# When the weight matrices are cast to bf16 for the scratch copy: all seven at the start, or two at the start and five behind the first K and V projections

## The chip, the cores and the metric

The kernel runs on all 8 cores of one Trainium2 chip. Each core computes two of the 16 sequences, and no core waits for another. The metric is the device time of the slowest core in microseconds.

A core has five engines with programs of their own: PE (matmuls), ACT (activations), DVE (vector work), POOL and SP (here both only issue transfers). They run side by side and meet through semaphores. 16 DMA engines do all transfers of the core.

## The reference, cut to what matters

For every sequence x of 2048 rows and 1024 columns, attention with 16 heads of 64, a residual and a layer norm, then a feed-forward block with a token shift, a residual and a layer norm:

```python
q, k, v = x @ Wq, x @ Wk, x @ Wv                  # per head
attn = softmax(q @ k.T / 65536)
x = layernorm(x + (attn @ v) @ WO)
xr = mu_r * x + (1 - mu_r) * x_prev               # x_prev: x one row earlier
xk = mu_k * x + (1 - mu_k) * x_prev
r = sigmoid(xr @ W_r.T)
x = layernorm(x + r * (square(relu(xk @ W_k.T)) @ W_v.T))
```

Seven weight matrices of 1024 x 1024 come in as float32 in one tensor `wts`, in the order WK, WV, WQ, WO, FR, FK, FV (0 to 6).

## The kernel before

All matmuls run in bf16. A weight matrix in bf16 fills one of three slots of 2 MB in SBUF. `WS[2]` holds WQ for the whole run. `WS[0]` and `WS[1]` are reloaded over and over, 36 times in all, from `wsc`, a bf16 copy of the matrices in device memory that the kernel makes itself at its start.

**The head.** POOL issues the load of a small constant and of WQ. Then a loop over m = 0 to 6 makes the scratch copy: POOL loads matrix m into `WS[m % 2]` with a cast from float32 to bf16, and SP writes the slot out to `wsc`. From m = 2 on POOL first waits until the slot's earlier write is done (counters `c_ws0` and `c_ws1`), and SP waits for each cast (`c_wc0`, `c_wc1`):

```python
for m in range(7):
    slot = WS[m % 2]
    if m >= 2:
        wait("g", c_wsx[m % 2], c_wsx[m % 2].n)
```

**Weight loads.** `load_weight(mat)` takes the slots 0 and 1 in turn. SP issues the load from `wsc`; the very first call waits for both counters of the scratch copy (`scratch_all`), and each call waits until the last matmul that reads the slot is done (`slot_free`).

**Per sequence.** `emit_kv` computes K and V for the whole sequence in four blocks of 512 rows, in the order 1, 2, 3, 0. Of each block it runs 64 matmuls for K with slot 0 and 64 for V with slot 1; results go through four PSUM banks and DVE writes them as bf16. The x blocks are loaded with a cast by POOL into two buffers in turn (`ABA`, `RG`), each issued during the K pass before it. Behind that come four stages t = 0 to 3, one for each block of 512 query rows: Q projection (`q_group`), then attention over 8 pairs of heads and 16 key tiles (`emit_attention`), in which PE computes scores, ACT the exps, PE the sums. Into the attention of stage t are woven the layer norm and the feed-forward work of stage t - 1 (`fillers`). The output projection of stage t - 1 (`emit_wo_pairs`, weights WO, residual from the tile `Y1`) stands at the start of stage t.

In stage t = 0 of the first sequence nothing is woven in. SP issues there the x tile for `Y1` and, behind it, the load of WO; POOL issues the x block for the next stage (`XRA`).

**What sets the order.** Each engine works through its own list in program order. A waiting POOL or SP therefore holds back every later transfer that it issues. The names that matter below: SP's list in the head is seven scratch writes, the reloads of WK and WV (`load_weight`), the x tile for `Y1`, then WO. POOL's list is WQ, seven casts, four x blocks of `emit_kv`, the block for `XRA`. Line 93 of the profile is every DMA issue, 99 every matmul, 109 every activation, 118 every vector operation, 84 every wait, since all are recorded by helpers.

Of the kernel before, what the change touches and what calls it, by code (L numbers as in the profile page):

```python
# [24 lines left out]
WK, WV, WQ, WO, FR, FK, FV = range(7)  # L25
# [8 lines left out]
def build_nc():  # L34
# [13 lines left out]
    def em(eng, fn):  # L48
        plan[eng].append(fn)

    def C(name):
        c = Cnt(name)
        sems[name] = c
        return c
# [6 lines left out]
    c_ws0 = C("c_ws0")  # L61
    c_ws1 = C("c_ws1")
# [9 lines left out]
    c_g = C("c_g")  # L72
# [7 lines left out]
    def wait(eng, c, val=None):  # L80
        v = c.n if val is None else val
        if v <= 0:
            return
        em(eng, lambda e, _n=c.name, _v=v: e.wait_ge(sem_handles[_n], _v))

    def bump(c, by=1):
        c.n += by
        return c.n

    def dma(eng, dst, src, c):  # L90
        n = bump(c, 16)
        em(eng, lambda e, _d=dst, _s=src, _n=c.name:
           e.dma_start(_d, _s).then_inc(sem_handles[_n], 16))
        return n

    def mm(out, lhsT, rhs, start, stop, tp=None, inc=None):
        n = bump(inc) if inc is not None else None
        def f(e, _o=out, _l=lhsT, _r=rhs, _st=start, _sp=stop, _tp=tp, _inc=inc):
            i = e.matmul(_o, _l, _r, start=_st, stop=_sp, tile_position=_tp,  # L99
                         skip_group_check=True)  # L100
            if _inc is not None:
                i.then_inc(sem_handles[_inc.name], 1)
        em("t", f)
        return n
# [10 lines left out]
    def vop(name, args, inc=None):  # L115
        n = bump(inc) if inc is not None else None
        def f(e, _nm=name, _a=args, _inc=inc):
            i = getattr(e, _nm)(*_a)  # L118
            if _inc is not None:
                i.then_inc(sem_handles[_inc.name], 1)  # L120
        em("v", f)
        return n
# [6 lines left out]
    with contextlib.ExitStack() as ctx:  # L129
# [54 lines left out]
        def next_bank():  # L184
            if use4[0]:
                b = pool4[hidx[0] % 4]
                hidx[0] += 1
            else:
                b = bG[gidx[0] % 2]
                gidx[0] += 1  # L190
            acquire(b)
            return b
# [96 lines left out]
        c_wc = [c_wc0, c_wc1]  # L289
        c_wsx = [c_ws0, c_ws1]  # L290
        c_w = [c_w0, c_w1]
        for m in range(7):
            slot = WS[m % 2]
            if m >= 2:
                wait("g", c_wsx[m % 2], c_wsx[m % 2].n)
            nld = dma("g", bass.AP(slot, 0, [[8 * D, 128], [D, 8], [1, D]]),
                      bass.AP(wts, m * D * D, [[D, 128], [128 * D, 8], [1, D]]),
                      c_wc[m % 2])
            wait("s", c_wc[m % 2], nld)
            dma("s", bass.AP(wsc, m * D * D, [[D, 128], [128 * D, 8], [1, D]]),  # L300
                bass.AP(slot, 0, [[8 * D, 128], [D, 8], [1, D]]), c_wsx[m % 2])

        wnext = [0]
        scratch_all = [(c_ws0, c_ws0.n), (c_ws1, c_ws1.n)]
# [3 lines left out]
        def load_weight(mat):  # L308
            si = wnext[0]
            wnext[0] = 1 - si  # L310
            if first_load[0]:
                wait("s", scratch_all[0][0], scratch_all[0][1])
                wait("s", scratch_all[1][0], scratch_all[1][1])
                first_load[0] = False
            fa = slot_free[si]
            if fa is not None:
                wait("s", fa[0], fa[1])
            n = dma("s", bass.AP(WS[si], 0, [[8 * D, 128], [D, 8], [1, D]]),
                    bass.AP(wsc, mat * D * D, [[D, 128], [128 * D, 8], [1, D]]),
                    c_w[si])  # L320
            return si, n
# [16 lines left out]
        for seq in range(NSEQ):  # L338
            def emit_kv(kv_fillers):
                use4[0] = True  # L340
                wk_si, wk_n = load_weight(WK)
                wv_si, wv_n = load_weight(WV)
                wk_last = wv_last = 0
                wait("t", c_w[wk_si], wk_n)
                wait("t", c_w[wv_si], wv_n)
                order = (1, 2, 3, 0)
                dsts = {1: ABA, 2: RG, 3: ABA, 0: RG}
                buf_free = {id(ABA): (c_g, xb_free[0]), id(RG): None}
                loads = {}

                def emit_load(tb):
                    buf = dsts[tb]
                    wait("g", c_xb, c_xb.n)
                    fa = buf_free[id(buf)]
                    if fa is not None:
                        wait("g", fa[0], fa[1])
                    loads[tb] = dma(
                        "g",
                        bass.AP(buf, 0, [[NCH * QT, 128], [QT, 8], [1, QT]]),
                        bass.AP(xT, seq * D * S + tb * QT,  # L360
                                [[S, 128], [128 * S, 8], [1, QT]]), c_xb)

                emit_load(1)
                for idx, tb in enumerate(order):
                    buf = dsts[tb]
                    nxb = loads[tb]
                    if tb == 0:
                        kv_nxb0[0] = nxb
                    wait("t", c_xb, nxb)
                    xbch = [buf[:, k * QT:(k + 1) * QT] for k in range(8)]  # L370
                    for hp in range(NHP):
                        b = next_bank()
                        for k in range(8):
                            mm(b.ap[:, :],
                               WS[wk_si][:, k * D + hp * 128: k * D + (hp + 1) * 128],
                               xbch[k], start=(k == 0), stop=(k == 7),
                               inc=(c_g if k == 7 else None))
                        wk_last = c_g.n
                        wait("v", c_g)
                        nv = vop("tensor_copy",  # L380
                                 (KTB[:, hp * S + tb * QT: hp * S + (tb + 1) * QT],
                                  b.ap[:, :]), inc=c_vg)
                        b.free = (c_vg, nv)
                    if kv_fillers:
                        kv_fillers.pop(0)()
                    if idx + 1 < len(order):
                        if buf_free[id(RG)] is None:
                            buf_free[id(RG)] = (c_g, c_g.n)
                        emit_load(order[idx + 1])
                    for tt in range(4):  # L390
                        for half in range(2):
                            b = next_bank()
                            for k in range(8):
                                mm(b.ap[:, :], xbch[k][:, tt * 128:(tt + 1) * 128],
                                   WS[wv_si][:, k * D + half * 512:
                                             k * D + half * 512 + 512],
                                   start=(k == 0), stop=(k == 7),
                                   inc=(c_g if k == 7 else None))
                            wv_last = c_g.n
                            kti = tb * 4 + tt  # L400
                            wait("v", c_g)
                            nv = vop("tensor_copy",
                                     (VTB[:, kti * D + half * 512:
                                          kti * D + half * 512 + 512],
                                      b.ap[:, :]), inc=c_vg)
                            b.free = (c_vg, nv)
                    if kv_fillers:
                        kv_fillers.pop(0)()
                    buf_free[id(buf)] = (c_g, wv_last)
                    xb_free[0] = wv_last  # L410
                slot_free[wk_si] = (c_g, wk_last)
                slot_free[wv_si] = (c_g, wv_last)
                while kv_fillers:
                    kv_fillers.pop(0)()
                use4[0] = False
# [4 lines left out]
            if prev is not None:  # L420
# [3 lines left out]
                kvf = [lambda: emit_ln1_head(prev),  # L424
                       lambda: (emit_ln_bcast_apply(prev, Y1)[0], emit_mix(prev))]
            emit_kv(kvf)

            wait("v", c_va, c_va.n)
# [646 lines left out]
```

## Time and profile before

| | us |
|---|---|
| median of two runs | 2720.14 (2711.89 and 2728.40) |
| the profiled execution, its own time | 2707.63 |
| its span on the slowest core (core 4) | 2706.1 |
| spans of the eight cores | 2693.5 to 2706.1 |
| PE busy | 2075.5 (77%) |
| ACT busy | 1244.6 (46%) |
| DVE busy | 835.1 (31%) |
| mean granted clock of PE | 0.897 |

Times within the trace count from the start of the span. "Busy" of PE and of the other engines is work only; waits and the issuing of transfers are not in it. The DMA share is the mean busy share of the 16 DMA engines and can come out a little above 1, since their packets overlap. A row such as "ws<-wts" names the destination and then the source. The load of a weight matrix or an x block with a cast counts by the bytes that it writes.

### The profile page before, as it was taken

Reading aid. Unit: us, or ns where it says so; the run is one execution under the profiler, and the core shown is the slowest. Engines: PE = TensorE matmul, PEld = TensorE weight load, DVE = VectorE, ACT = ScalarE, POOL = GpSimd, SP = SyncE. Lnnn points to the kernel's source line nnn. Section 1 sums busy time; section 2 is a strip of 40 time slices with the busy share of each in tenths; the row PEclk is TensorE's granted clock in tenths of the full one; section 3 lists DMA queues with packets and bytes.
Section 4 is the critical chain, followed back from the end, with each engine's and each line's share of the span. In section 5 each row is a group of like instructions: output and inputs, shape, how many; then the busy total and the mean of one; then the engine's idle time right before and its main releaser. Section 6 shows DMA issues by size and latency. Waiting matters only on the chain.

```text
span 2706.1 us, 29989 instructions; the slowest of 8 cores (2693.5 to 2706.1 us)
## 1 busy us (share of the span) xinstructions
PE 2075.5 (77%) x10062; PEld 709.2 (26%) x10176; DVE 835.1 (31%) x1369; ACT 1244.6 (46%) x1441; POOL 20.1 (1%) x27
## 2 busy tenths in 40 slices
PE   0019988788878897889669888788988798879835
PEld 0004322222322232223224222222322232223212
DVE  0003200240524052405264014240434133423355
ACT  0000277375537653665200656457445655565511
POOL 0000000000000000000000000000000000000000
PEclk9999988898989898889779999898988898889867
DMA  9984100000410041003222013100230013001201
GB/s 175 205 196 63 63 1 1 32 1 32 109 63 1 32 109 63 1 32 94 78 31 48 31 63 79 63 1 1 75 110 19 1 63 110 31 1 63 94 31 63
DMA packets 85136, 157.24 MB, mean 58 GB/s; under 512 B 1984, under 2 KB 16384, under 8 KB 84992
## 3 DMA queue, kind: packets, MB, share of 16 engines
q1 hardware_dynamic: 53264, 107.07, 12.4%
q0 software_dynamic: 23024, 31.47, 8.0%
q10 hardware_dynamic: 8704, 16.78, 1.7%
q8 instruction: 91, 1.49, 0.2%
q14 instruction: 53, 0.43, 0.1%
HBM read 155.31 MB, written 31.46 MB: 69 GB/s over the span
## 4 chain that ended last, share of the span: by engine, by line
PE 54%; ACT 19%; DVE 11%; DMA 7%; issue 7%; ACTq 1%; DVEq 0%; POOL 0%; SPq 0%; POOLq 0%
PE psg L99 28%; ACT pb L109 13%; PE pspv L99 11%; PE psden L99 10%; ACT lta L109 4%; DMA ws<-wts 4%; PE psa L99 3%; PE psb L99 3%; DMA wsc<-ws 3%; DVE xka L118 2%; DVE stv L118 2%; DVE rg L118 1%; DVE xra L118 1%; DVE recb L118 1%; ACT rcr L109 1%
## 5 line engine op out<-in xcount | busy, mean ns | idle before, releaser
L109 ACT ACTIVATE pb<-psa 128x1024 bf16<-128x1024 f32 x512 | 522.6, 1021 | 396.6 <-PE psa L99 395.4
L109 ACT ACTIVATE pb<-psb 128x1024 bf16<-128x1024 f32 x512 | 523.5, 1022 | 362.7 <-PE psden L99 192.6
L99 PE MATMUL pspv<-pb,vtb 128*64 128x512 bf16 x2048 | 427.5, 426 | 23.0 <-DVE aba L118 22.9
L99 PE MATMUL psden<-pb,cstb 128*32 128x512 bf16 x2048 | 410.5, 409 | 0.0
L99 PE MATMUL psg<-xra,ws 128*128 128x512 bf16 x1264 | 343.2, 422 | 9.3 <-issue 8.6
L99 PE MATMUL psa<-qtb,ktb 64*128 64x512 bf16 x1024 | 213.6, 405 | 144.6 <-ACT pb L109 84.6
L118 DVE TENSOR_TENSOR aba<-pspv,rsb 128x512 bf16<-128x512 f32 x64 | 44.3, 692 | 767.9 <-ACT rsb L109 766.8
L99 PE MATMUL psg<-aba,ws 128*128 128x512 bf16 x373 | 95.4, 409 | 218.7 <-DMA ws<-wsc 190.9
L99 PE MATMUL psb<-qtb,ktb 64*128 64x512 bf16 x1024 | 207.6, 399 | 62.4 <-ACT pb L109 62.4
L99 PEld LDWEIGHTS pspv<-pb,vtb 128*64 128x64 bf16 x2048 | 110.7, 109 | 283.6 <-issue 283.6
L99 PEld LDWEIGHTS psg<-xra,ws 128*128 128x128 bf16 x1320 | 128.6, 105 | 199.5 <-issue 94.6
L99 PEld LDWEIGHTS psden<-pb,cstb 128*32 128x32 bf16 x2048 | 93.8, 94 | 250.3 <-issue 250.3
L109 ACT ACT_TABLE_LOAD x1 | 1.3, 1283 | 306.4 <-PE psa L99 306.4
L99 PEld LDWEIGHTS psa<-qtb,ktb 64*128 64x128 bf16 x1024 | 53.0, 93 | 301.8 <-issue 300.9
L99 PE MATMUL psg<-rcr,cstf 64*128 64x512 f32 x128 | 83.4, 736 | 57.9 <-ACT rcr L109 57.9
L99 PEld LDWEIGHTS psg<-aba,ws 128*128 128x128 bf16 x384 | 39.7, 104 | 273.8 <-issue 236.0
L99 PEld LDWEIGHTS psb<-qtb,ktb 64*128 64x128 bf16 x1024 | 52.6, 93 | 214.8 <-issue 214.8
L99 PE MATMUL psg<-xka,ws 128*128 128x512 bf16 x465 | 105.6, 379 | 2.3 <-issue 2.2
L118 DVE CAST qtb<-psg 128x512 bf16<-128x512 f32 x60 | 41.5, 691 | 173.6 <-PE psg L99 173.6
L118 DVE CAST ktb<-psg 128x512 bf16<-128x512 f32 x32 | 22.0, 691 | 230.3 <-PE psg L99 229.3
L118 DVE TENSOR_SCALAR stv<-psg 128x512 f32<-128x512 f32 x30 | 20.7, 691 | 223.4 <-PE psg L99 223.4
L109 ACT ACTIVATE rsb<-psg 128x512 f32<-128x512 f32 x64 | 38.2, 597 | 98.9 <-PE psg L99 98.9
(113 smaller groups left out, 1695.9 us busy)
## 6 DMA issues: line engine op xcount, KB each, us to landing
ws<-wsc SPq DMA_DIRECT2D x36, 2048.0 KB, 10.1
ws<-wts POOLq DMA_DIRECT2D x8, 2048.0 KB, 25.8
y<-xT SPq DMA_DIRECT2D x8, 2048.0 KB, 13.2
outT<-outb ACTq DMA_DIRECT2D x32, 512.0 KB, 4.0
wsc<-ws SPq DMA_DIRECT2D x7, 2048.0 KB, 12.5
xra<-xT POOLq DMA_DIRECT2D x6, 1024.0 KB, 12.2
aba<-xT POOLq DMA_DIRECT2D x4, 1024.0 KB, 13.6
rg<-xT POOLq DMA_DIRECT2D x4, 1024.0 KB, 8.9
```

The source lines that it names most:

```text
L99: i = e.matmul(_o, _l, _r, start=_st, stop=_sp, tile_position=_tp, skip_group_check=True)
L109: i = e.activation(_o, _i, _f, scale=_s, bias=_b)
L118: i = getattr(e, _nm)(*_a)
```

## The change

The loop becomes a function, `emit_wcast(m)`, with the same two transfers and one more wait. It is called for matrices 0 and 1 (WK and WV) at the old place, and for 2 to 6 behind the K and V projections of the first sequence. Those projections no longer call `load_weight`: they read WK and WV in the slots into which they were cast, and PE waits for the two casts. The casts of matrices 2 to 6 wait, besides the slot's earlier scratch write, for the last K matmul (slot 0) or the last V matmul (slot 1). The scratch counters on which the first `load_weight` waits, now that of WO in stage t = 0, are set again behind the last cast. For the second sequence nothing changes.

```diff
-        for m in range(7):
+        kv0_gate = [0, 0]
+
+        def emit_wcast(m):
             slot = WS[m % 2]
             if m >= 2:
                 wait("g", c_wsx[m % 2], c_wsx[m % 2].n)
+                wait("g", c_g, kv0_gate[m % 2])
             nld = dma("g", bass.AP(slot, 0, [[8 * D, 128], [D, 8], [1, D]]),
                       bass.AP(wts, m * D * D, [[D, 128], [128 * D, 8], [1, D]]),
                       c_wc[m % 2])
             wait("s", c_wc[m % 2], nld)
             dma("s", bass.AP(wsc, m * D * D, [[D, 128], [128 * D, 8], [1, D]]),
                 bass.AP(slot, 0, [[8 * D, 128], [D, 8], [1, D]]), c_wsx[m % 2])
+            return nld
+
+        wk0_n = emit_wcast(0)
+        wv0_n = emit_wcast(1)
...
             def emit_kv(kv_fillers):
                 use4[0] = True
-                wk_si, wk_n = load_weight(WK)
-                wv_si, wv_n = load_weight(WV)
+                if seq == 0:
+                    wk_si, wv_si = 0, 1
+                    wait("t", c_wc[0], wk0_n)
+                    wait("t", c_wc[1], wv0_n)
+                else:
+                    wk_si, wk_n = load_weight(WK)
+                    wv_si, wv_n = load_weight(WV)
+                    wait("t", c_w[wk_si], wk_n)
+                    wait("t", c_w[wv_si], wv_n)
                 wk_last = wv_last = 0
-                wait("t", c_w[wk_si], wk_n)
-                wait("t", c_w[wv_si], wv_n)
...
                 slot_free[wk_si] = (c_g, wk_last)
                 slot_free[wv_si] = (c_g, wv_last)
+                if seq == 0:
+                    kv0_gate[0], kv0_gate[1] = wk_last, wv_last
+                    for m in range(2, 7):
+                        emit_wcast(m)
+                    scratch_all[0] = (c_ws0, c_ws0.n)
+                    scratch_all[1] = (c_ws1, c_ws1.n)
```

## Rows read from the trace of the kernel before

**Rows 1.** The page's chain that ended last, by engine and by line.

```profile
PE 54%; ACT 19%; DVE 11%; DMA 7%; issue 7%; ACTq 1%; DVEq 0%; POOL 0%; SPq 0%; POOLq 0%
PE psg L99 28%; ACT pb L109 13%; PE pspv L99 11%; PE psden L99 10%; ACT lta L109 4%; DMA ws<-wts 4%; PE psa L99 3%; PE psb L99 3%; DMA wsc<-ws 3%; DVE xka L118 2%; DVE stv L118 2%; DVE rg L118 1%; DVE xra L118 1%; DVE recb L118 1%; ACT rcr L109 1%
```

**Rows 2.** That chain in order of time: start us, us, what.

```profile
3.14 29.92 DMA ws<-wts
...
33.13 18.38 DMA wsc<-ws
...
116.20 19.45 DMA wsc<-ws
...
136.18 22.45 DMA ws<-wts
...
158.69 11.86 DMA wsc<-ws
...
171.10 19.60 DMA ws<-wsc
190.70 0.24 issue
190.94 5.24 PE psg L99 x16
```

**Rows 3.** Busy time by stretch (the busy engines, clock, DMA share, GB/s).

```profile
0.00:191.00 191.00, 0.06 (x1) 0.09 (x2) 3.50 (x1) 0.00 (x0) 8.78 (x14) 1.00 1.00 197
191.00:305.00 114.00, 113.44 (x510) 51.11 (x520) 44.38 (x72) 0.00 (x0) 3.49 (x4) 1.00 0.32 67
194.00:337.00 143.00, 139.83 (x662) 59.99 (x672) 49.91 (x80) 20.13 (x21) 3.49 (x4) 1.00 0.28 61
337.00:500.00 163.00, 139.78 (x711) 39.57 (x713) 6.82 (x10) 119.78 (x133) 0.00 (x0) 0.85 0.00 1
207.00:217.00 10.00, 9.95 (x47) 4.53 (x47) 3.80 (x6) 0.00 (x0) 0.87 (x1) 1.00 0.68 107
305.00:313.00 8.00, 6.70 (x38) 2.25 (x38) 2.08 (x3) 4.55 (x5) 0.00 (x0) 1.00 0.75 262
```

**Rows 4.** SP's and POOL's issues in order of time: start, us, engine, what.

```profile
48.92 0.36 SPq L93 DMA_DIRECT2D wsc<-ws  x1
158.69 0.36 SPq L93 DMA_DIRECT2D wsc<-ws  x1
289.50 0.36 SPq L93 DMA_DIRECT2D ws<-wsc  x1
171.77 6.57 SPq L93 DMA_DIRECT2D y<-xT  x1
137.04 0.88 POOL L93 DMA_DIRECT2D aba<-xT  x1
```

**Rows 5.** Issues of short stretches: KB, us to landing (at 48.92, 137.04, 171.1, 171.8, 207.09).

```profile
wsc<-ws SPq DMA_DIRECT2D x1, 2048.0 KB, 12.0
aba<-xT POOLq DMA_DIRECT2D x1, 1024.0 KB, 29.2
ws<-wsc SPq DMA_DIRECT2D x1, 2048.0 KB, 19.6
y<-xT SPq DMA_DIRECT2D x1, 2048.0 KB, 24.2
rg<-xT POOLq DMA_DIRECT2D x1, 1024.0 KB, 9.6
```

**Rows 6.** Spans and clocks, and core 0's first matmuls in order of time.

```profile
core 0: 2704.1 us, clock 0.897
core 4: 2706.1 us, clock 0.897
187.85 5.80 PE L99 MATMUL psg<-aba,ws 128*128 128x512 bf16 x16 [187.85 <-DMA ws<-wsc]
```

**Rows 7.** POOL's issues in order of time, with the idle time before each.

```profile
52.05 0.88 POOL L93 DMA_DIRECT2D ws<-wts  x1 [47.14 <-DMA wsc<-ws]
...
93.75 0.87 POOL L93 DMA_DIRECT2D ws<-wts  x1 [31.42 <-DMA wsc<-ws]
...
136.18 0.87 POOL L93 DMA_DIRECT2D ws<-wts  x1 [31.49 <-DMA wsc<-ws]
...
207.09 0.87 POOL L93 DMA_DIRECT2D rg<-xT  x1 [69.17 <-PE psden L99]
```

**Rows 8.** PE and DVE in order of time, at the end of stage t = 0.

```profile
492.25 2.86 PE L99 MATMUL psg<-aba,ws 128*128 128x512 bf16 x7 [2.23 <-DVE aba L118]
497.02 0.69 DVE L118 TENSOR_TENSOR outb<-psg,y 128x512 f32<-128x512 f32 x1 [5.50 <-PE pspv L99]
507.04 1.89 PE L99 MATMUL psg<-xra,ws 128*128 128x512 bf16 x8
```

**Rows 9.** ACT in order of time, first attention steps.

```profile
308.60 1.02 ACT L109 ACTIVATE pb<-psb 128x1024 bf16<-128x1024 f32 x1
...
316.66 1.02 ACT L109 ACTIVATE pb<-psa 128x1024 bf16<-128x1024 f32 x1
```

## The prediction

> **What bounds the kernel now.** I read the page's chain by engine and line first [rows 1]: PE holds 54% of the chain, but "DMA ws<-wts" 4% and "DMA wsc<-ws" 3% are on it too, and a transfer on the chain is time in which nobody computes. The chain in order of time shows where [rows 2]: from 3.14 us to 190.94 us it is only transfers, a weight matrix into SBUF, out to the scratch copy `wsc`, the next one in, four times over, then the reload of two matrices, and only then the first matmul at 190.94. The stage table says the same [rows 3]: in 0 to 191 us PE is busy 0.06 us and the 16 DMA engines are full (share 1.00); in 191 to 305 us, the K and V projections of sequence 0, PE is busy 113.44 of 114 us. So the head is bound by DMA, the projections behind it by PE, and the attention stages behind those by PE and ACT in turn. PE is in fixed program order and everything behind the first matmul waits for it directly or indirectly, so an earlier first matmul moves the rest as a block, unless something in that block then meets a transfer that comes too late.
>
> **The change part by part.**
>
> Removed from the head: the casts of matrices 2 to 6, their scratch writes, and the reload of matrices 0 and 1. The K and V projections take their weights straight from the slots into which they were cast. What they now wait for is three transfers: WK, WV and the first x block.
>
> WK is in at 33.1 us and WV at 48.9: SP waits for exactly these landings before it issues each scratch write, and the issues stand at 33.13 and 48.92 [rows 2, 4]. Up to there the new program issues the same transfers in the same order, so both numbers carry over.
>
> The first x block now follows WV directly on POOL's queue. The trace has the same pair: the block is issued at 137.04 behind the last matrix, that matrix is in by 158.69 (the issue of its scratch write), and the block lands 29.2 us after its own issue, at 166.2 [rows 4, 5]. That is 7.5 us behind the matrix, with a scratch write of 2 MB running beside it as it will in the new head. One thing is different: at 48.9 the scratch write of WK still runs, until 33.13 + 18.38 = 51.5 us [rows 2], which at worst puts 2.6 us of full DMA ahead of the block. So the block lands between 48.9 + 7.5 = 56.4 and 59.0; I take 58, towards the upper end since the engines are full, and the first matmul there. (A landing releases PE within 0.24 us: 171.10 + 19.60 against 190.94 [rows 2].) Gain on core 4: 190.9 - 58 = 132.9 us. On core 0, which starts at 187.85 and has a span of 2704.1, the gain is 129.9, and its span becomes 2574.2; core 4's becomes 2706.1 - 132.9 = 2573.2 [rows 6]. The slowest core then stands at about 2574.
>
> The HBM page of the Trainium skill (HBM Reference, Specifications) gives about 358 GB/s a core with both cores of a pair streaming. As an estimate from that page, three float32 matrices and one block, 14.7 MB, would be in after 41 us, at about 44, and the sum would be 14 us lower; the trace does not agree, it has only the three matrices (12.6 MB) in at 48.9, some 280 GB/s, and I go by the trace.
>
> The K and V projections themselves: 114 us as before. Their later x blocks are issued by POOL ahead of the moved casts, so nothing new is queued before them. The only transfer still running at their start is the scratch write of WV, 12 us long from 48.92 on [rows 5]; the second x block is issued 16 us behind the first matmul [rows 7], at about 74, when this write is over. Cost 0.
>
> Moved behind the projections: five casts and five scratch writes. POOL's cast of matrix 2 waits for the last K matmul, which today releases SP's reload at 289.50 [rows 4], so 289.5 - 132.9 = 156.6. The first of them has the engines nearly alone; from then on the pair period is that of the head, 41.7 and 42.4 us from matrix 2 to 4 to 6 (POOL's issues at 52.05, 93.75 and 136.18) [rows 7]. Only slot 1 opens later, with the last V matmul at 303.1 - 132.9 = 170, and matrix 3 must be queued at 170 instead of 9 us behind matrix 2; it still goes in while matrix 2 is written out. In: matrix 2 at about 173 (WV took 48.92 - 33.13 = 15.8 us), written by 192 (18.4 to 19.5 us), matrix 4 issued at 192, matrix 6 at 234 (one period), in at 256.5 (22.45 us), written at 268.4 (11.86 us) [rows 2].
>
> What is queued behind them. On SP: the x tile for `Y1`, which today is issued at 171.77 and needs 24.2 us, now goes out at 257 and is in at 281; then WO, which waits for both scratch counters (268.4) and needs 19.6 us, in at 288 [rows 4, 5]. On POOL: the x tile for the next stage (`XRA`), behind the cast of matrix 6, issued at 235 and in by 235 + 29.2 = 264. Who waits: the output projection of stage t = 0 has its first matmul at 492.25 today, so 359.3; the first sum with `Y1` is at 497.02, so 364.1; the first matmul on `XRA` at 507.04, so 374.1 [rows 8]. Slack: 71 us for WO, 83 for `Y1`, 110 for `XRA`. The cover is the attention stage t = 0, some 185 us with no transfer of its own (DMA share 0.00 in 337 to 500 us [rows 3]). Cost 0; with the cover gone it would be 1 us for every us beyond 71.
>
> Beside other work: the moved traffic fills the DMA engines (share 1.0) for about 112 us of attention. No stretch of before has both at full. The nearest: 207 to 217 us has DMA at 0.68 with PE busy 9.95 of 10; 305 to 313 us has DMA at 0.75 in the first attention steps [rows 3], and the exps there take 1.02 us each, as at 316.66 us with that load over [rows 9]. Bound below: nothing. A gain is excluded, since traffic lends no engine anything. Bound above: 8 us, 5% of the stage, for what a share of 1.0 might do that 0.75 doesn't. I take 0, since the row at 0.75 shows none.
>
> Sum: span 2706.1 gives 2574 for the slowest core; around it lay 2707.6 - 2706.1 = 1.5 us, so 2575.7 by the profiled execution. The two runs of before are 2711.9 and 2728.4, median 2720.1, some 4 to 21 us above the profiled one; less 132 the median would give 2588. Between the two I say **2580**.
>
> **The rivals.**
>
> *The first x block comes after the scratch write, not beside it.* If the engines favour the write of WV (over at about 61.5), the block of 9.6 us [rows 5] lands near 71, 13 us later: 2593. For it: the engines are full. Against it: at 158.69 to 170.6 the same two ran side by side and the block was in first.
>
> *The clock.* Granted clock is 1.00 from 194 to 337 us and 0.85 from 337 to 500 [rows 3], that is a mix of 2.4 and 1.2 GHz that begins 143 us behind PE's start. If that full stretch is earned by the 191 us of idling within the program, 58 us of idling would earn 58/191 of it, 44 us. The other 70 us of projections at 0.85 would take 12 us more, and the attention up to the old turning point some 4 more: 2596. Against it: PE was idle before the program too, and the stretch may simply count from PE's start, in which case it moves along.
>
> *The scratch copy is late.* Decides when WO lands past 359, that is when casts and writes take over 183 us instead of 112. At half the rate (224) WO lands at 400 and it costs 41 us: 2621; at a third (336) 153 us, and the whole gain is gone. Against it: rates are those of the head, where the engines did nothing else either.
>
> *Slower than before: PE and ACT suffer from the full DMA engines.* Place: the attention stage from 157 to 268 us. Each per cent is 1.1 us; the gain of 132 is eaten when the 112 us of work take 244, a factor of 2.2, and it is over 2% slower (2774 and up) from a factor of 2.7. Against it: at a share of 0.68 PE lost nothing [rows 3]. The Trainium skill (SBUF — State Buffer, SBUF: two separate sides) holds engine ports and DMA ports to be separate, so that neither slows the other; by that rule this rival would have no chance at all, and no run here shows it at a share of 1.0.
>
> **How the numbers follow.** My forecast 0.81, its own range 2563 to 2596 (landing 56.4 to 59.0, contention 0 to 8, and the 13 us between the two bases). Late x block 0.06, clock 0.06, late scratch copy 0.04, engines slowed 0.03. A range of 2562 to 2604 takes in the first three and leaves out the rest and the odd tail. About 2% is what a measurement of this kernel can tell from no change, so faster means under 2666: forecast, x block, clock, and half of the scratch rival, 0.95; within 2%: the other half and a third of the last, 0.03; slower 0.02.
>
> **What would show it.** First matmul at 56 to 60 us on core 4, released by the x block and not by a weight. PE busy over 99% in the next 114 us. Clock 1.00 until about 201 us. POOL's casts from 156 on with periods near 42 us, DMA share near 1.0 until 268, then WO at about 288. The first output projection at 359, not released by a DMA. From there on every stage 133 us earlier with its old length. I am wrong if the output projection waits for WO or `Y1`, if the clock falls long before 201 us, or if the exps between 157 and 268 us come further apart than they do now between 305 and 400.

## The result

| | before | after |
|---|---|---|
| time, median | 2712.31 us (10 runs) | 2584.01 us (11 runs) |
| profiled execution: its time, its span | 2707.63, 2706.1 | 2583.61, 2582.1 |
| ratio of the undisturbed runs | 1 | 0.953, 95% interval 0.9505 to 0.9555 |

The kernel is 128 us faster, 4.7%. The forecast was 2580. In some executions the cores of one die run at a lower clock and take longer; the two medians hold these too (without them they are 2711.9 and 2583.6), the ratio and all times below do not.

The page of the changed kernel, chain by engine: the share of DMA fell from 7% [rows 1] to 1%, and a 2% part appears that the chain cannot name. It is the wait for the first x block, 61 us long, as the row of PE shows further down.

```profile
PE 58%; ACT 20%; DVE 11%; issue 7%; another core or an unknown queue 2%; ACTq 1%; DMA 1%; DVEq 0%; POOLq 0%
```

The chain in order of time on core 3, the slowest (start us, us, what). Where before stood casts, writes and a reload one behind the other up to 190.94 [rows 2], one wait is left:

```profile
0.00 61.45 another core or an unknown queue
61.45 0.14 issue
61.58 6.21 PE psg L99 x16
```

Matmuls in order of time, the first on cores 3 and 4. The bracket names the idle time before and what ended it: the x block in `ABA`, no weight.

```profile
61.58 6.21 PE L99 MATMUL psg<-aba,ws 128*128 128x512 bf16 x16 [61.58 <-DMA aba<-xT]
61.94 5.01 PE L99 MATMUL psg<-aba,ws 128*128 128x512 bf16 x16 [61.94 <-DMA aba<-xT]
```

Stages of the changed kernel on core 3 (start and end, length, busy PE, weight loads, DVE, ACT, POOL, clock, DMA share, GB/s). They answer to [rows 3]: first the K and V projections with the end of the head, then the stretch of full clock, then attention with the moved casts beside it.

```profile
58.00:172.00 114.00, 110.42 (x500) 49.55 (x501) 42.70 (x62) 0.00 (x0) 3.50 (x4) 1.00 0.31 52
61.00:204.00 143.00, 141.08 (x660) 60.35 (x660) 49.91 (x80) 15.63 (x16) 5.24 (x6) 1.00 0.45 82
204.00:370.00 166.00, 142.18 (x727) 40.12 (x726) 6.82 (x10) 124.34 (x138) 2.62 (x3) 0.87 0.59 124
```

PE is busy in 110.42 of the 110.42 us that remain of the first stretch behind 61.58. The clock is 1.00 for 143 us from the start of PE and 0.87 in the stretch behind it; before, it was 1.00 from 194 to 337 and then 0.85 [rows 3]. Read in steps of 1 us, it first falls 147 to 149 us behind the first matmul on the eight cores, and 146 to 148 us in the kernel before.

POOL's and SP's issues on core 3 in order of time. They answer to [rows 4, 7]: the casts now stand behind the projections, a matrix pair every 38.1 and 42.7 us, and the reload of WO is issued at 278.44.

```profile
4.86 0.91 POOL L93 DMA_DIRECT2D aba<-xT  x1
...
161.57 0.87 POOL L93 DMA_DIRECT2D ws<-wts  x1 [40.57 <-PE psden L99]
175.38 0.87 POOL L93 DMA_DIRECT2D ws<-wts  x1 [12.94 <-PE psden L99]
199.63 0.87 POOL L93 DMA_DIRECT2D ws<-wts  x1 [23.37 <-DMA wsc<-ws]
210.85 0.87 POOL L93 DMA_DIRECT2D ws<-wts  x1 [10.35 <-DMA wsc<-ws]
242.36 0.87 POOL L93 DMA_DIRECT2D ws<-wts  x1 [30.63 <-DMA wsc<-ws]
243.22 0.88 POOL L93 DMA_DIRECT2D xra<-xT  x1
```

```profile
50.78 0.36 SPq L93 DMA_DIRECT2D wsc<-ws  x1
264.80 0.36 SPq L93 DMA_DIRECT2D wsc<-ws  x1
265.25 0.57 SPq L93 DMA_DIRECT2D y<-xT  x1
278.44 1.39 SPq L93 DMA_DIRECT2D ws<-wsc  x2
```

The end of stage t = 0 on core 4, PE in order of time: the output projection is still released by DVE and not by a transfer, with the same idle time of 2.23 us as in [rows 8].

```profile
360.53 3.19 PE L99 MATMUL psg<-aba,ws 128*128 128x512 bf16 x7 [2.23 <-DVE aba L118]
```

**Where the time went.** Split each core's span at its first matmul. The head was 181.2 to 190.9 us long on the eight cores and is 60.2 to 62.4 now. The rest, from first matmul to the end, was 2512.4 to 2516.6 us, on average 2514.6, and is 2513.4 to 2520.5, on average 2517.0. So the head gave 121 to 129 us on a core, and the rest took 2.4 us back on average, more on core 3, where 2512.9 became 2520.5, and on core 7, where 2513.9 became 2520.5. The average rest of the kernels below that differ only in the head lies between 2512.4 and 2516.8, so 2.4 us is within what one execution and another differ by.

The spans and clocks of these two cores after the change:

```profile
core 3: 2582.1 us, clock 0.888
core 4: 2576.8 us, clock 0.891
```

Core 3's 7.6 us lie behind stage t = 0: from its first matmul to the output projection it took 487.74 - 187.94 = 299.8 us before and 362.16 - 61.58 = 300.6 after, and from there to the end 2213.1 and 2219.9. In that later part the two programs issue the same work, and core 4 shows no such difference (rest of 2515.2 before, 2514.9 after). The same 1300 us near the end, before and after on core 3 (columns of [rows 3]), show what it is:

```profile
1400.00:2700.00 1300.00, 1067.42 (x5140) 361.06 (x5140) 447.91 (x743) 638.27 (x746) 3.50 (x4) 0.88 0.16 49
1272.00:2572.00 1300.00, 1075.97 (x5140) 361.89 (x5140) 444.54 (x738) 639.02 (x746) 3.49 (x4) 0.87 0.15 48
```

PE is busy 8.6 us longer with the same number of matmuls, at a granted clock of 0.87 instead of 0.88; on core 7 it is 8.8 us with the same two clocks. So these microseconds go with the granted clock. Why it was lower on these two cores is not shown; I count it to the scatter between cores.

### The profile page after: what moved, and what is told of

It reads as the page before. It is cut to its first block, busy times and chain, and to the rows that moved or that the text cites. A ratio compares the mean times of both kernels' runs of the same rounds, so it can differ in the third digit from the quotient of the medians.

```text
span 2582.1 us, 30106 instructions; the slowest of 8 cores (2573.9 to 2582.1 us)
## 1 busy us (share of the span) xinstructions
PE 2103.9 (81%) x10176; PEld 710.7 (28%) x10176; DVE 834.9 (32%) x1369; ACT 1245.8 (48%) x1441; POOL 20.1 (1%) x27
## 4 chain that ended last, share of the span: by engine, by line
PE 58%; ACT 20%; DVE 11%; issue 7%; another core or an unknown queue 2%; ACTq 1%; DMA 1%; DVEq 0%; POOLq 0%
PE psg L99 29%; ACT pb L109 13%; PE pspv L99 11%; PE psden L99 11%; ACT lta L109 5%; PE psa L99 4%; PE psb L99 3%; DVE xka L118 2%; DVE stv L118 2%; DVE rg L118 2%; DVE xra L118 1%; DVE recb L118 1%; ACT rcr L109 1%; DVE y L118 1%
## 5 line engine op out<-in xcount | busy, mean ns | idle before, releaser
L99 PE MATMUL psg<-xra,ws 128*128 128x512 bf16 x1320 | 351.4, 419 | 0.3 <-issue 0.3
L109 ACT ACTIVATE lta<-psg 128x512 f32<-128x512 f32 x60 | 35.8, 596 | 65.0 <-PE psg L99 64.4
```

Of the source, the lines that this page charges most:

```text
L109: i = e.activation(_o, _i, _f, scale=_s, bias=_b)
```

## The experiments

Every kernel below starts from the changed one. "First matmul" is that of core 4 unless said otherwise, and a single core scatters by some 2 us, so averages over the eight cores are given where it matters.

### One part undone: the reload

```diff
-                if seq == 0:
-                    wk_si, wv_si = 0, 1
-                    wait("t", c_wc[0], wk0_n)
-                    wait("t", c_wc[1], wv0_n)
-                else:
-                    wk_si, wk_n = load_weight(WK)
+                wk_si, wk_n = load_weight(WK)
...
                     scratch_all[1] = (c_ws1, c_ws1.n)
+                    first_load[0] = True
```

> The changed kernel with one part undone: the casts of matrices 2 to 6 stay behind the first projections, but WK and WV are loaded once more from the scratch copy before the projections start, as in the kernel before. Theory (the head is a chain of transfers, each part worth its own transfers): both scratch writes are done near 64 us, the two reloads take about 20 us, so the first matmul stands near 84 instead of 61 us and the time is 2584 + 22 = 2606. So of the 128 us, about 106 come from moving the five casts and 22 from not reloading. Rival (the time is set by the body, the head is half hidden): under 5 us difference, 2585 to 2589. The stretch of full clock should again end 143 us behind the first matmuls, near 230 us, if it counts from PE's start; if idling within the program earns it, it would be longer than in the changed kernel.

Measured: 2604.2 us (one execution), first matmul at 81.94, released by the reload:

```profile
63.97 0.99 SPq L93 DMA_DIRECT2D ws<-wsc  x2
```

```profile
81.94 6.08 PE L99 MATMUL psg<-aba,ws 128*128 128x512 bf16 x16 [81.94 <-DMA ws<-wsc]
```

The head is additive: on core 4 the first matmul is 20.0 us later, and the time is 20.2 us more. Over the eight cores the first matmul is 21.9 us later (83.1 against 61.2) and the rest behind it 1.9 us shorter (2515.1 against 2517.0). So some 20 to 22 of the 128 us come from reading WK and WV where they were cast, and the other 106 to 108 from moving the five casts. Its busy table has clock 1.00 from 85 to 228 us and 0.87 behind:

```profile
85.00:228.00 143.00, 140.47 (x662) 60.18 (x672) 49.91 (x80) 19.40 (x20) 6.14 (x7) 1.00 0.46 87
228.00:300.00 72.00, 60.75 (x316) 16.61 (x314) 2.77 (x4) 56.11 (x63) 1.75 (x2) 0.87 1.02 218
```

In steps of 1 us the clock first falls 146 to 149 us behind the first matmul on the eight cores, as it does with first matmuls near 61 and near 187. The idling inside the program earns nothing, and the clock rival falls. That the stretch counts from PE's start, as I had argued, does not follow: up to there PE does the same work in all three kernels, so the fall can just as well belong to a place in the program, some 35 us behind the last V matmul. The kernels below in which PE has to wait speak for the place: where the waits add up to 12 to 16 us, it falls 163 to 167 us behind the first matmul.

### What the moved traffic costs: none of it, and twice of it

```diff
-                    for m in range(2, 7):
+                    for m in ():
...
-                    bass.AP(wsc, mat * D * D, [[D, 128], [128 * D, 8], [1, D]]),
+                    bass.AP(wsc, (mat % 2) * D * D, [[D, 128], [128 * D, 8], [1, D]]),
```

> The changed kernel with the moved work left out: no casts and scratch writes of matrices 2 to 6; every later weight load reads the scratch copy of WK or WV instead of its own matrix, so the computed values are those of other weights, while all matmuls, loads and waits stay. It shows what the moved traffic costs the attention beside it. Theory (full DMA engines slow nobody): first matmul near 61 us, first output projection 299 to 301 us behind it as in the changed kernel, time 2580 to 2585. Rival (they slow PE and ACT): the output projection comes 3 us or more earlier against the first matmul, time under 2578.

```diff
-                    for m in range(2, 7):
+                    for m in (2, 3, 4, 5, 2, 3, 4, 5, 6, 3):
```

> The changed kernel with ten casts and scratch writes behind the first projections instead of five (2, 3, 4, 5 done twice, then 6 and 3 again), so twice the traffic and a later WO. It prices the rival 'scratch copy late' and the rival 'engines suffer from full DMA engines'. Theory (cover with slack): the last write ends near 380 us, WO is in near 392, the output projection of stage t = 0 would start at 361 and so waits about 30 us: 2614. The attention steps in between keep their length to 1%. Rival (full DMA engines slow PE and ACT): the attention stage itself becomes longer, by 5 us or more beside the wait.

Measured: 2583.3 and 2584.5 us without the casts, 2614.5 and 2616.8 with twice as many. The attention of stage t = 0 on core 4, the same 187 us in three kernels: no casts, five casts (the change), ten casts. The columns are those of [rows 3].

```profile
165.00:352.00 187.00, 165.37 (x868) 49.40 (x866) 15.34 (x30) 134.38 (x146) 0.00 (x0) 0.92 0.06 22
```

```profile
165.00:352.00 187.00, 164.99 (x865) 49.32 (x866) 14.64 (x29) 135.44 (x148) 4.36 (x5) 0.91 0.71 151
```

```profile
165.00:352.00 187.00, 164.99 (x860) 49.10 (x861) 14.64 (x29) 134.41 (x147) 8.74 (x10) 0.90 1.02 194
```

The DMA share goes from 0.06 over 0.71 to 1.02, and PE does 868, 865 and 860 matmuls, ACT 146, 148 and 147 activations. From first matmul to output projection core 4 takes 361.66 - 63.83 = 297.8 us without the casts and 360.53 - 61.94 = 298.6 with them. A single core scatters by more than that. Over the eight cores the rest behind the first matmul is 2516.6 us on average without and 2517.0 with, and PE needs from its first matmul to the end of its work before the output projection 298.2 us on average with no casts, 298.5 with five, 298.5 with ten (the wait for WO taken off) and 298.8 in the kernel before, with 295.9 to 299.7 on single cores. So full DMA engines slow neither engine by as much as 1 us in this stage. (By the Trainium skill, SBUF — State Buffer, SBUF: two separate sides, engine and DMA ports cannot contend; here the trace agrees, up to a share of 1.02.)

The kernel without casts is not faster as a whole, since its first matmul came later, at 63.8 (63.4 against 61.2 over the eight cores). SP had no casts to wait for and issued the 2 MB x tile for `Y1` at 49.2, beside the x block; I take that for the cause, it was not tried by itself.

The price of a late scratch copy shows in the ten casts. The reload of WO is issued at 383.64 on core 4, and the longest waits of PE there are

```profile
PE psg L99 <- DMA aba<-xT: 61.3, 1, 61.3
PE psg L99 <- DMA ws<-wsc: 38.1, 1, 38.1
```

The second is 27.9 us on core 3, where that reload is issued at 373.02, and 26.1 to 40.8 us over the eight cores. The time is 30 to 33 us up. WO's issue moved by 105.7 us on core 4 (277.95 to 383.64), of which 38.1 became a wait, and by 94.6 on core 3 (278.44 to 373.02), of which 27.9 did. So 67.6 and 66.7 us cost nothing: the slack that I had put at 71 us is measured on two cores. Between the two, 11.1 us more of delay became 10.2 us more of wait.

### What sets the first matmul: the queue ahead of the x block, and the writes beside it

```diff
-        n_wq_res = dma("g", bass.AP(WS[2], 0, [[8 * D, 128], [D, 8], [1, D]]),
-                       bass.AP(wts, WQ * D * D, ...), c_wqr)
+        n_wq_res = [0]
...
                 emit_load(1)
+                if seq == 0:
+                    n_wq_res[0] = dma("g", bass.AP(WS[2], 0, ...), bass.AP(wts, WQ * D * D, ...), c_wqr)
```

> The changed kernel with POOL's load of WQ moved behind WK, WV and the first x block. Theory (the first matmul waits for everything that stands before the x block in POOL's queue): one matrix less before it, 14 to 16 us, first matmul near 46 us, time 2584 - 15 = 2569. Rival (the x block's landing is set by the scratch writes beside it and not by the queue ahead): the first matmul stays within 5 us of 61, time 2580 to 2584.

Measured: 2569.8 us (one execution), first matmul at 53.2 on core 4 and 50.8 on core 3. The time fell by 14 as expected, but not for the reason expected: over the eight cores the first matmul fell by 9.7 us only (61.2 to 51.5), and the other 4.6 are the rest behind it (2517.0 to 2512.4), which this edit should not change. That the time came out right is luck. The queue ahead counts, but a matrix less ahead is not 15 us. The scratch write of WK starts sooner too (20.51 instead of about 33) and so runs beside all of WV and the block; that this took the missing 5 us is argued and was not tried.

Next the writes. `emit_wwrite(m)` below is the scratch write alone, the `dma("s", ...)` of the removed lines:

```diff
-            wait("s", c_wc[m % 2], nld)
-            dma("s", bass.AP(wsc, m * D * D, ...), bass.AP(slot, 0, ...), c_wsx[m % 2])
+            if m >= 2:
+                wait("s", c_wc[m % 2], nld)
+                emit_wwrite(m)
...
                 emit_load(1)
+                if seq == 0:
+                    wait("s", c_xb, loads[1])
+                    wait("s", c_wc[0], wk0_n)
+                    emit_wwrite(0)
+                    wait("s", c_wc[1], wv0_n)
+                    emit_wwrite(1)
```

> The changed kernel with SP holding the scratch writes of WK and WV until the first x block is in. It prices the term that I had too small, the x block at 61.4 where 58 was forecast: WV came at 50.8 to 51.2 (forecast 48.9) and the block 10.7 us behind it (forecast 9.1). Theory (the writes take their share of the DMA engines from WV and the block): without them WV is in near 47 and the block near 55, first matmul 6 us earlier, time 2578. Rival (the block is bound by its own reads, the writes fit into gaps): first matmul within 1.5 us of 61, 2584.

Measured: 2572.9 and 2574.5 us, first matmul at 50.92, with the writes issued right behind:

```profile
50.92 1.00 SPq L93 DMA_DIRECT2D wsc<-ws  x2
```

11 us earlier on core 4 and 10.4 over the eight cores, where 6 were expected: the scratch writes of WK and WV, which nobody needs before stage t = 0, held up the start by that much. The rival that they fit into gaps falls. The landings of WV and the block on core 4, counted from their issues at about 4.0 and 4.9, divide it, first in the changed kernel, then here:

```profile
ws<-wts POOLq DMA_DIRECT2D x1, 2048.0 KB, 47.2
aba<-xT POOLq DMA_DIRECT2D x1, 1024.0 KB, 56.9
```

```profile
ws<-wts POOLq DMA_DIRECT2D x1, 2048.0 KB, 41.0
aba<-xT POOLq DMA_DIRECT2D x1, 1024.0 KB, 45.9
```

WV is in 6.2 us sooner, and the block follows it by 5.8 us instead of 10.6.

### Using it: a shorter head

The first diff builds on `wq_last`, in which WQ has left the head of POOL's list; each further one shows only what is new against the kernel ahead of it. First WK, the x block, WV and WQ in that order, with PE waiting for WV only before the first V pass:

```diff
-        wv0_n = emit_wcast(1)
+        wv0_n = [0]
...
                 emit_load(1)
+                if seq == 0:
+                    wv0_n[0] = emit_wcast(1)
+                    n_wq_res[0] = dma("g", ...)          # WQ
...
+                    if seq == 0 and idx == 0:
+                        wait("t", c_wc[1], wv0_n[0])
                     for tt in range(4):
```

> As in wq_last, but POOL's order is WK, first x block, WV, WQ, and PE waits for WV only before the first V pass. Theory: WK is in near 20 us and the block near 30, first matmul at 30. WV is in near 47, just before the V pass at 48. But the second x block is issued near 47 behind WQ, lands past 70, and is needed at 59: PE stalls about 12 us there. Sum: 2584 - 31 + 12 = 2565. Rival (no such stall, the queues serve the block first): 2553. Rival on the other side (the stall also lowers the clock): above 2570.

Measured: 2567.2 and 2568.8 us, first matmul at 31.0. PE's waits on core 4 show what took the place of the old one: the second x block, queued behind WQ, and a little WV.

```profile
PE psg L99 <- DMA rg<-xT: 11.6, 1, 11.6
...
PE psg L99 <- DMA ws<-wts: 2.9, 1, 2.9
```

The stall breaks the stretch of full clock too; these are the projections around it:

```profile
31.00:64.00 33.00, 29.68 (x126) 12.74 (x128) 10.60 (x16) 0.00 (x0) 0.88 (x1) 1.00 1.03 193
64.00:78.00 14.00, 2.73 (x7) 1.05 (x8) 0.47 (x1) 0.00 (x0) 0.87 (x1) 0.67 0.68 141
78.00:190.00 112.00, 109.92 (x520) 46.83 (x528) 38.85 (x64) 16.27 (x17) 3.50 (x4) 0.99 0.48 87
```

Then WQ behind the second x block:

```diff
                         emit_load(order[idx + 1])
+                        if seq == 0 and idx == 0:
+                            n_wq_res[0] = dma("g", ...)  # WQ
```

> POOL's order WK, first x block, WV, second x block (issued behind the first K pass), WQ; PE waits for WV before the first V pass. The difference to wk_x_wv_wq is that WQ stands behind the second block. Theory (the stall of 11.6 us there was the block queued behind WQ): first matmul at 30 as there, no wait for the second block, up to 3 us of wait for WV, time 2568 - 12 = 2556. The stretch of full clock, which there was broken by the stall after 34 us, runs 143 us from PE's start again. Rival (the block is slow whatever stands before it, since the scratch writes run beside it): the wait stays over 8 us, 2565.

Measured: 2556.4 to 2556.9 us, first matmul at 30.7. The wait for the second block fell from 11.6 to 4.5 us on core 4, not to nothing, and that for WV to 1.3; over the eight cores it fell from 8.6 to 12.9 us to 2.1 to 6.1 on four of them and to none on the other four. The time is as expected. The clock was not whole again on core 4: it is 0.94 from 30 to 69 us. On core 1, with a wait of 2.1 us, it is 1.00 there.

Next the scratch writes held until WV is in (`emit_wwrite` as above, behind waits for `c_wc[0]` and `c_wc[1]`):

> As wq_after_x2, and SP holds both scratch writes until WV is in. Theory (the writes cost the loads their share): first matmul near 28 instead of 30, no wait for WV (in near 42, needed at 46), but both writes now run beside the second block, issued near 45 and needed near 59; a write and a block side by side took 10 to 12 us, so it is just in time. Time 2556 - 5 = 2551. Rival (two writes beside the second block delay it past 59): a wait of up to 6 us there and no gain, 2556.

Measured: 2559.2 and 2559.3 us, no gain; 2576.7 in the execution of the trace, in which cores 0 and 1 took some 20 us more than the other six. First matmul at 25.9, 4.8 us earlier, but

```profile
PE psg L99 <- DMA rg<-xT: 8.9, 1, 8.9
```

instead of 4.5, and 6.0 to 8.9 us on all eight cores: the rival was right. The block was issued at 42.15 and both writes at 37.97, and they ran side by side. What the writes no longer cost the first block they cost the second.

So the second block has to be issued sooner; its buffer is free from the start. It goes out as soon as the first is in, and WQ behind it:

```diff
+                    emit_load(order[1])
+                    n_wq_res[0] = dma("g", ...)          # WQ
...
-                        emit_load(order[idx + 1])
+                        if not (seq == 0 and idx == 0):
+                            emit_load(order[idx + 1])
```

> POOL's order WK, first x block, WV, second x block issued as soon as the first is in (its buffer is free from the start), then WQ; SP holds both scratch writes until WV is in. The last kernel showed that the earlier first matmul (26 instead of 30 us) was given back to a wait of 8.9 us for the second block, which was issued only behind the first K pass. Theory (the block was late because it was issued late and then shared with two writes): it now follows WV directly, is in near 48 to 52, needed at 55, no wait; first matmul at 26; time 2557 - 4.5 - 4.5 - 1.3 = 2547. Rival (some other transfer takes its place: the third block behind WQ, needed near 84): a new wait of 3 us or more at the third block, 2550 or above.

Measured: 2546.0 us in the profiled execution, 2549.5 in the median; the four executions lie between 2546.0 and 2562.4; ratio to before 0.940, interval 0.931 to 0.950. That interval covers the 0.943 of `wq_after_x2`, so the step of 7 to 10 us between the two kernels is shown by the waits in the traces and not by the ratios. First matmul at 26.88, and no other transfer stands among PE's waits until the attention, on any of the eight cores. POOL issued the block at 27.28:

```profile
27.28 0.88 POOL L93 DMA_DIRECT2D rg<-xT  x1 [22.38 <-DMA aba<-xT]
```

Last, the block ahead of WK, and WK in two halves of 512 columns with a counter each, PE waiting for the second half before the fifth group:

```diff
+                    for h, c_ in ((0, c_wka), (1, c_wc0)):
+                        wkh.append(dma("g",
+                            bass.AP(WS[0], h * 512, [[8 * D, 128], [D, 8], [1, 512]]),
+                            bass.AP(wts, h * 512, [[D, 128], [128 * D, 8], [1, 512]]), c_))
...
+                        if seq == 0 and idx == 0 and hp == 4:
+                            wait("t", c_wc0, wkh[1])
```

> As x2_at_once, but the first x block goes ahead of WK, and WK comes as two casts of 512 columns each, so that PE begins with the first half. Theory: block in near 11, first half of WK near 18, first matmul at 18 instead of 26; WV in near 38 but needed at 34 (18 + 16): 4 us of wait; net 4 us faster than x2_at_once, 2543. Rival (rows of half the length load more slowly, or the waits for WV and the third block eat the gain): within 2 us of x2_at_once or slower.

Measured: 2545.7 to 2547.1 us, ratio 0.937, interval 0.929 to 0.946; not to be told from the kernel before it. First matmul at 19.98, 6.9 us earlier, of which 3.2 go into a wait for WV before the first V pass, where 4 were expected; the second half of WK is not waited for. The casts behind the projections are issued at 122.37 instead of 126.94, so 4.6 us reach that point on core 4; at the end of the run core 4 is 2 us ahead (2542.1 to 2544.1) and the slowest core not at all. Where they went was not tried.

## Why the prediction was right, point by point

**The head is a chain of transfers and the rest moves as a block.** Right. The rest behind the first matmul stayed within 2.4 us on average, and the reload alone gave back 20 us at the end for 20 to 22 us at the start.

**WK and WV carry over at 33.1 and 48.9.** WK right (33.42 on core 3); WV came at 50.8 on core 3 and 51.2 on core 4, 2 us later, and at 50.1 instead of 48.7 on average over the eight cores. Up to there the issues differ only in the x block queued behind WV; the write of WK beside it ran longer too, on core 4 23.2 us instead of 18.4. Which of the two did it was not tried. A part can be scatter: `no_casts` has the same head up to there and has WV in at 48.7 on core 4.

**The x block, 9.1 us behind WV, at 58.** Too small by 3.6 us: it came at 61.4, outside the stretch of 56.4 to 59.0 that I had given. Of the 3.6, WV's own landing is 1.9 and the block behind it 1.6 (10.7 us instead of 9.1). I took 7.5 us from a block that ran beside one write and added at most 2.6 for the tail of the other. That tail was longer: on core 4 the write of WK ran until 55.9, 4.7 us past WV. `write_later` measured what both writes cost the start: 11 us. The row from which I worked held such a write already, so its price could not be seen in it.

**The slowest core.** I forecast a span of 2574.2 for it, from core 0 with a rest of 2516.2. It was core 3 with a rest of 2520.5. So the miss of 7.9 us in the span is 3.6 for the block and 4.3 for the scatter of the rest. That 2580 was only 4 us off is luck: by the profiled execution alone the sum was 2575.7, 8 us short, and the 4 us that I added came from the scatter of two runs of the kernel before (2711.9 and 2728.4), not from anything in the change.

**Projections at full clock, 114 us.** Right: matrix 2's cast waits for the last K matmul and goes out at 161.57 on core 3, 100.0 us behind the first matmul; the same matmul released SP's reload 99.1 us behind it there before. On core 4 it is 98.8 against 98.6.

**Moved casts and slack.** Forecast: casts from 156.6, WO's reload issued at 268.4 with 71 us of slack. Measured 161.6 and 278.4; relative to the first matmul, 216.9 instead of 210.4. The slack held, and `double_casts` found its edge, at 67 us, within 5 us of the sum. The two do not quite mean the same: WO's issue was 6.5 us later than forecast against the first matmul, so by my sum some 64 would have been left.

**Full DMA engines cost nothing.** Right, and now shown at a share of 1.02 to under 1 us over eight cores, where before had only rows at 0.68 and 0.75. The exps between 170 and 340 us took 1.02 us each with none, five and ten casts.

**The rivals.** Late x block: the measured landing is 3.6 us from the forecast and nearly 10 from this rival. Clock: falls, by three starts; my counter-argument, that the stretch counts from PE's start, is not shown. I had also begun the stretch at 194, 3 us behind the first matmul at 190.94. Late scratch copy: its mechanism is real, its condition was not met. Slower: falls. The estimate from the HBM page of the Trainium skill (HBM Reference, Specifications), a block at about 44 us, did not come about, not even with the writes held back, where it was in at 50.9.

## What to carry to other kernels

Where the first matmul waits for transfers, list what stands ahead of each input in its queue and what runs beside it, and ask of each when it is needed: five casts and a reload were 128 us, and the order of WQ, WV, an x block and two writes another 34 to 38. Each time the first wait is shortened, look for the next input in program order; here it took the gain twice, until its own issue was moved. The transfers that moved under compute here cost nothing that could be measured as long as their slack held, and beyond it each microsecond of delay was about a microsecond of wait.

## What the runs showed of the hardware that I had not expected

- Writing 4 MB of scratch copy beside the casting loads of the head delayed their end by 11 us (61.9 to 50.9), nearly twice what I had expected.
- The clock first falls 146 to 149 us behind the first matmul, on all eight cores, whether that matmul is near 50, 61, 83 or 187 us. With waits of PE in between it falls later: 163 to 167 us behind it in `wk_x_wv_wq` (waits of 12 to 16 us), 150 to 154 in `wk_halves` (2 to 4 us), where the kernel without such waits, `x2_at_once`, has 146 to 152. So the fall keeps closer to a place in the work than to a time since PE began; what in the attention brings it on was not tried.
- A stall of PE of 11.6 us (`wk_x_wv_wq`) brought 0.67 for 14 us and then 0.99 for the next 112; one of 4.5 us (`wq_after_x2`, core 4) brought a mean of 0.94 over 39 us.
